# Gated cross-attention with a quantised feed-forward on one core: contexts in another row order, hand-written closing lists, and a different order of the first loads

## The chip, the cores and the metric

The kernel runs on one core of a Trainium2 chip. The metric is the device time of one launch in microseconds.

## What is computed

For 32 batches, queries `x` [32, 112, 256] attend to contexts `ctx_1024` [32, 375, 256], and a feed-forward with ternary weights and 8-bit activations follows. Cut to what matters:

```python
q  = layernorm(layernorm(x)) @ Wq * (1 + side) + side      # 16 heads of 64
k, v = split(layernorm(ctx) @ Wkv)
x  = x + tanh(g_xattn) * softmax(q k^T / 8) v @ Wout
h  = gelu(bitlinear(layernorm(x), w1, b1))
x  = x + tanh(g_ffn) * bitlinear(h, w2, b2)
# bitlinear: rmsnorm, activations rounded to 8 bits by the row's maximum, weights to -1, 0, 1
```

The softmax and the sum over the keys do not depend on the order of the 375 context rows.

## The kernel before

Products that need more than half precision are split into a high and a low f16 part, and `three` (L755 to L760) adds three products. Each batch goes through these steps, whose names are those of the order tables:

- LD, LX (SP): load the context into `ctx_in` [125, 3, 256] and the queries into `x_in` [112, 256]. BA, BB, BS (VectorE): their statistics; LNA (POOL): the scales; LNW (ScalarE): the normalised rows.
- Z0, Z1, ZX (TensorE): transposes into a work bank; ZF, ZXF (ScalarE) and ZS, ZXS (POOL): the high and low parts.
- K0 to K7, V00 to V12, Q0, Q1 (TensorE): projections, each into one of three PSUM work banks that go round in the order of TensorE's list. KH and VH (ScalarE) write the high part, KL and VL (VectorE) the low part and free the bank; QF (ScalarE) and QS (POOL) do it for the queries.
- For each of 8 pairs of heads: S (TensorE) scores, M (VectorE) maximum, E (ScalarE) exponential, PH (ScalarE or VectorE) high part, PL (POOL) low part, T (SP) the DMA transpose `pt<-pn`, A (TensorE) probabilities times values. N (VectorE) normalises four heads.
- OO, OH, OT: transpose the attention output and split it.

The 3584 rows of all batches are then taken as 28 tiles of 128 rows, numbered 0 to 27: WO (output projection), X1 and XST (residual, statistics), RM1, SC1, XR, XQ (quantise), XD (SP, DMA transpose of `xq`), XTE (VectorE, clips), F0 and F1 (first feed-forward product), HE0 and HE1, GE (gelu), SQ, HMX (maximum), RM2, SC2, HR, HQ (quantise), HD (DMA transpose of `hid_q`), HTE (clips), F2, YE, ST (store). In the tables tile t is written as a batch number: 31 is tile 27, 30 is 26, 29 is 25, 28 is 24, 27 is 23.

No scheduler decides anything. Each engine runs the list that `sequence` (L139) makes: FIRST[engine] for the opening rounds, then ORDER[engine] once per batch with offsets, until the batches run out. An engine waits on semaphores in front of a step, and all that stands behind in its list waits too. SP's list is the order of all DMAs on the one queue. The weights are loaded on SP at the start; those needed later (wout, w1, w2, the biases and gates, 3.7 MB) are issued inside `load` for batch 1, right after its context.

Of the kernel before, what the change touches and what calls it, by code (L numbers as in the profile page):

```python
# [4 lines left out]
F16 = mybir.dt.float16  # L5
ALU = mybir.AluOpType
# [3 lines left out]
B, SQ, D = 32, 112, 256  # L10
# [3 lines left out]
P = 128  # L14
# [33 lines left out]
ORDER, FIRST = {}, {}  # L48
# [20 lines left out]
]  # L69
# [20 lines left out]
]  # L90
# [48 lines left out]
def sequence(engine):  # L139

    done = set(FIRST[engine])
    steps = FIRST[engine] + [(name, it + off) for it in range(START, END) for name, off in ORDER[engine]
                             if 0 <= it + off < B and (name, it + off) not in done]
    return [(name, b - b // 8 - 1 if name in TOKEN_STEPS else b) for name, b in steps if b % 8 or name not in TOKEN_STEPS]
# [26 lines left out]
def build(nc, x, ctx, fside, g_x, g_f, ln1w, ln1b, ln2w, ln2b, wq, wkv, wout, w1, b1, w2, b2, out):  # L171
    from contextlib import ExitStack
    with ExitStack() as st:
# [25 lines left out]
        ident = sb("ident", [P, P])  # L199
# [70 lines left out]
        def _(sp):  # L270
            sp.dma_start(ctx_in[:], ctx[0].rearrange("(t p) d -> p t d", p=TP)).then_inc(ctx_loaded, 16)
# [11 lines left out]
            def load(b):  # L283
                if b == 0:
                    return
                sp.wait_ge(ctx_normed, b)
                sp.dma_start(ctx_in[:], ctx[b].rearrange("(t p) d -> p t d", p=TP)).then_inc(ctx_loaded, 16)
                if b == 1:
                    sp.dma_start(gates[:, 0:1], g_x.partition_broadcast(P)).then_inc(small_in, 16)
                    sp.dma_start(gates[:, 1:2], g_f.partition_broadcast(P)).then_inc(small_in, 16)  # L290
                    sp.dma_start(b2_row[:], b2.partition_broadcast(P)).then_inc(small_in, 16)
                    sp.dma_start(wout_f, wout.rearrange("(k p) n -> p k n", p=P)).then_inc(wout_in, 16)
                    sp.dma_start(w1_f, w1.rearrange("(k p) n -> p k n", p=P)).then_inc(w1_in, 16)
                    sp.dma_start(w2_f, w2.rearrange("(k p) n -> p k n", p=P)).then_inc(w2_in, 16)
                    sp.dma_start(b1_row[:], b1.partition_broadcast(P)).then_inc(small_in, 16)
# [30 lines left out]
            for name, b in sequence("SP"):  # L326
                if name[0] == "T":
                    turn(b, int(name[1]))
                if name == "XD":
                    turn_quantised(b)  # L330
                if name == "HD":
                    turn_hidden(b)
                if name == "LD":
                    load(b)
# [571 lines left out]
```

## Time and profile before

| | us |
|---|---|
| median of 3 runs | 1146.59 (1146.12 to 1147.98) |
| the profiled execution | 1148.09 |
| its span in the profile | 1146.2 |
| TensorE busy (93% of the span) | 1069.4 |
| ScalarE, VectorE, POOL busy | 974.0, 943.3, 776.7 |

The profile's span runs from the first to the last instruction of one execution; the profiled execution's own time is 1.9 us more. Busy time of TensorE counts matmuls with modelled ends. A row of a timeline gives the start, the duration, the engine, the line of the kernel, the operation, what is written and read, and in brackets how long the engine had been idle and what ended that.

### The profile page before, as it was taken

What the parts mean: (1) busy time and instruction counts of PE and PEld (TensorE: products, weight loads), DVE (VectorE), ACT (ScalarE), POOL (GpSimd) and SP (SyncE); (2) the same over time, 40 slices, a digit from 0 to 9 for tenths busy, and PEclk for the clock granted to TensorE, in tenths of its full rate; (3) what the DMA queues carried; (4) which work ended last, traced back from release to release, by engine and by line L of the source; (5) the groups of instructions that cost most, each with busy time, mean ns of one, the idle gap of its engine ahead of it and who ended that gap; (6) DMA issues with size and microseconds to landing.
All of it is one profiled execution on the core that took longest, in us unless ns stands there. A gap on an engine that the chain in (4) does not pass through costs nothing.

```text
span 1146.2 us, 32095 instructions
## 1 busy us (share of the span) xinstructions
PE 1069.4 (93%) x11890; PEld 735.4 (64%) x11890; DVE 943.3 (82%) x2108; ACT 974.0 (85%) x1866; POOL 776.7 (68%) x837
## 2 busy tenths in 40 slices
PE   3788999999999999999999999999999999999972
PEld 1455666776676676767666676776677667766650
DVE  3686788888889888888888878888988878988863
ACT  4677789999999979999999979999999979998861
POOL 3466577776767777676777666767777776777631
PEclk9899999999999999999999999999999999999975
DMA  8155745676786656778865776676667676755451
GB/s 273 50 97 91 115 87 108 125 114 113 117 137 108 103 113 124 117 108 125 119 111 110 127 115 104 112 136 101 111 126 114 117 122 111 120 107 103 105 103 30
DMA packets 418840, 129.72 MB, mean 113 GB/s; under 512 B 392480, under 2 KB 417536, under 8 KB 418688
## 3 DMA queue, kind: packets, MB, share of 16 engines
q1 hardware_dynamic: 418688, 127.68, 63.5%
q8 instruction: 97, 1.59, 0.6%
q14 instruction: 55, 0.45, 0.1%
HBM read 26.71 MB, written 3.67 MB: 27 GB/s over the span
## 4 chain that ended last, share of the span: by engine, by line
PE 71%; ACT 9%; DMA 6%; issue 6%; POOL 3%; DVE 3%; POOLq 1%; SPq 0%; DVEq 0%; ACTq 0%
PE work L757 15%; PE work L759 14%; PE work L758 14%; PE ps_s L776 10%; DMA pt<-pn 6%; PE ps_o L757 3%; PE ps_o L759 3%; PE ps_o L758 3%; ACT prob L538 2%; PE work L839 2%; PE work L857 2%; ACT L538 2%; ACT q_f L504 2%; PE work L863 2%; PE work L830 2%
## 5 line engine op out<-in xcount | busy, mean ns | idle before, releaser
L379 POOL TENSOR_TENSOR pn<-prob,pn 112x750 f16<-112x750 f32 x256 | 399.5, 1566 | 123.1 <-ACT pn L548 111.6
L538 ACT ACTIVATE prob<-ps_s,neg_max 112x375 f32<-112x375 f32 x512 | 265.2, 573 | 16.7 <-DVE neg_max L680 13.6
L680 DVE TENSOR_REDUCE neg_max<-ps_s 112x2 f32<-112x750 f32 x256 | 237.4, 928 | 23.6 <-PE ps_s L776 23.5
L757 PE MATMUL ps_o<-v_h,pt 128*128 128x65 f16 (+1 forms) x1536 | 168.3, 195 | 18.3 <-DMA pt<-pn 14.6
L757 PE MATMUL work<-z,wkv_h 128*128 128x375 f16 x512 | 168.6, 329 | 15.2 <-DVE k_l L605 8.1
L461 ACT ACTIVATE k_h<-work 128x375 f16<-128x375 f32 x256 | 121.4, 487 | 61.2 <-PE work L759 55.6
L605 DVE SCALAR_TENSOR_TENSOR k_l<-work,k_h 128x375 f16<-128x375 f32 x256 | 136.3, 540 | 40.7 <-ACT k_h L461 40.5
L758 PE MATMUL ps_o<-v_l,pt 128*128 128x65 f16 (+1 forms) x1536 | 168.0, 193 | 0.0
L759 PE MATMUL ps_o<-v_h,pt 128*128 128x65 f16 (+1 forms) x1536 | 168.0, 194 | 0.0
L759 PE MATMUL work<-z,wkv_l 128*128 128x375 f16 x512 | 167.4, 327 | 0.0
L758 PE MATMUL work<-z,wkv_h 128*128 128x375 f16 x512 | 167.0, 326 | 0.0
L757 PEld LDWEIGHTS ps_o<-v_h,pt 128*128 128x128 f16 (+1 forms) x1536 | 143.8, 98 | 34.1 <-DMA pt<-pn 18.7
L758 PEld LDWEIGHTS ps_o<-v_l,pt 128*128 128x128 f16 (+1 forms) x1536 | 143.2, 99 | 9.2
L757 PE MATMUL work<-wkv_h,z 128*128 128x512 f16 (+1 forms) x384 | 146.7, 382 | 1.4 <-DVE k_l L605 1.1
L759 PE MATMUL work<-wkv_h,z 128*128 128x512 f16 (+1 forms) x384 | 145.5, 379 | 0.0
L758 PE MATMUL work<-wkv_l,z 128*128 128x512 f16 (+1 forms) x384 | 145.4, 379 | 0.0
L759 PEld LDWEIGHTS ps_o<-v_h,pt 128*128 128x128 f16 (+1 forms) x1536 | 143.2, 97 | 0.0
L605 DVE SCALAR_TENSOR_TENSOR v_l<-work,v_h 128x512 f16<-128x512 f32 (+1 forms) x192 | 128.3, 681 | 6.7 <-ACT v_h L461 6.1
L461 ACT ACTIVATE v_h<-work 128x512 f16<-128x512 f32 (+1 forms) x192 | 115.6, 603 | 9.7 <-PE work L759 8.4
L548 ACT ACTIVATE pn<-prob 112x750 f16<-112x750 f32 x128 | 107.7, 842 | 0.1
L504 ACT ACTIVATE q_f<-work,side_add,side_mul 128x112 f32<-128x112 f32 x256 | 93.9, 467 | 6.0 <-PE work L759 6.0
L776 PE MATMUL ps_s<-k_h,q_h 64*112 64x375 f16 x512 | 88.7, 343 | 1.0 <-POOL q_l L387 0.7
(125 smaller groups left out, 2729.7 us busy)
## 6 DMA issues: line engine op xcount, KB each, us to landing
ctx_in<-in_ctx SPq DMA_DIRECT2D x32, 375.0 KB
pt<-pn SPq DMA_TRANSPOSE x256, 3.5
x_in<-in_x SPq DMA_DIRECT2D x32, 112.0 KB, 3.4
x_res<-in_x SPq DMA_DIRECT2D x28, 128.0 KB, 4.1
out<-y SPq DMA_DIRECT2D x28, 128.0 KB, 2.0
stage<-in_wkv SPq DMA_DIRECT2D x2, 1024.0 KB, 9.6
stage<-in_w SPq DMA_DIRECT2D x2, 1024.0 KB, 11.8
stage<-in_wq SPq DMA_DIRECT2D x1, 1024.0 KB, 9.1
```

Source lines behind the costliest of these rows:

```text
L379: g.tensor_tensor(buf[:, 1, :, 0:SK], prob[:, p % 2], buf[:, 0, :, 0:SK], ALU.subtract).then_inc(p_lo, 1)
L461: a.activation(dst, src, ACT.Identity, scale=1.0 / W_SCALE).then_inc(hi_done, 1)
L504: i = a.activation(q_f[:, c, :], work[:, BANK[job], m * SQ:(m + 1) * SQ], ACT.Identity, bias=add, scale=mul)
L538: i = a.activation(prob[:, p % 2, h, :], ps_s[0:SQ, 2 * (p % 2) + h, 0:SK], ACT.Exp, bias=neg_max[:, 2 * (p % 2) + h:2 * (p % 2) + h + 1])
L548: a.activation(pn[g % PBUF][:, 0, :, 0:SK], prob[:, p % 2], ACT.Identity).then_inc(p_hi_act, 1)
L605: v.scalar_tensor_tensor(out=dst, in0=src, scalar=1.0 / W_SCALE, in1=hi_part, op0=ALU.mult, op1=ALU.subtract).then_inc(evacuated[BANK[job] ...
L680: v.tensor_reduce(neg_max[:, 2 * (p % 2):2 * (p % 2) + 2], ps_s[0:SQ, 2 * (p % 2):2 * (p % 2) + 2, 0:SK], X, ALU.max, negate=True).then_in ...
L757: t_.matmul(dst, sh, mh, start=(n == 0), stop=False)
L758: t_.matmul(dst, sh, ml, start=False, stop=False)
L759: i = t_.matmul(dst, sl, mh, start=False, stop=(n == len(pairs) - 1))
L776: i = t_.matmul(ps_s[0:SQ, 2 * (p % 2) + h, 0:SK], q[r, p, :], k[r, p, :], start=(n == 0), stop=(n == 2))
L830: i = t_.transpose(w[:, t * TP:(t + 1) * TP], ctx_n[:, t, c * P:(c + 1) * P], ident[0:TP, 0:TP])
```

## The change

Five edits:

1. A context is loaded with three rows to a partition (row 3p + t in partition p, one piece of 3 KB) where partition p held rows p, 125 + p and 250 + p (three pieces of 1 KB).
2. The late weights are issued behind the queries of batch 1. The new list has LX of batch 1 ahead of LD of batch 1.
3. New FIRST lists for all five engines.
4. A LAST list for each engine, which sets the order of the closing rounds step by step.
5. For the last tile alone, `xq` and `hid_q` are transposed by TensorE into a PSUM bank (XT, HT), with a new f16 identity, and VectorE clips out of PSUM. The DMA transposes XD and HD of this tile are gone.

```diff
-            sp.dma_start(ctx_in[:], ctx[0].rearrange("(t p) d -> p t d", p=TP)).then_inc(ctx_loaded, 16)
+            sp.dma_start(ctx_in[:], ctx[0].rearrange("(p t) d -> p t d", p=TP)).then_inc(ctx_loaded, 16)
...
+            def load_queries(b):
+                if b > 0:
+                    sp.wait_ge(ctx_normed, b)
+                    sp.dma_start(x_in[:], x[b]).then_inc(x_loaded, 16)
                 if b == 1:
+                    load_late_weights()
...
-    done = set(FIRST[engine])
+    done = set(FIRST[engine] + LAST[engine])
     steps = FIRST[engine] + [(name, it + off) for it in range(START, END) for name, off in ORDER[engine]
-                             if 0 <= it + off < B and (name, it + off) not in done]
+                             if 0 <= it + off < B and (name, it + off) not in done] + LAST[engine]
...
+LAST["PE"] = [
...
+    ("K6", 31), ("A6", 30), ("F2", 27), ("A7", 30), ("S6", 31), ("S7", 31), ("OO1", 30), ("V01", 31),
+    ("V00", 31), ("WO", 30), ("F0", 29), ("F1", 29), ("V11", 31), ("A0", 31), ("V12", 31), ("V10", 31),
+    ("A1", 31), ("A2", 31), ("A3", 31), ("A4", 31), ("A5", 31), ("F2", 28), ("A6", 31), ("A7", 31),
+    ("OO0", 31), ("OO1", 31), ("F0", 30), ("F1", 30), ("WO", 31), ("F2", 29), ("XT", 31), ("F0", 31),
+    ("F1", 31), ("F2", 30), ("HT", 31), ("F2", 31),
+]
...
-                if name == "XTE":
+                if name == "XTE" and b == NT - 1:
+                    dve.wait_ge(full[BANK["XT", b]], USE["XT", b])
+                    v.tensor_scalar(xqt[:].rearrange("p c q -> p (c q)"), work[:, BANK["XT", b], :].bitcast(F16)[:, 0:KC * P],
+                                    -QMAX - 1, QMAX, ALU.max, ALU.min).then_inc(evacuated[BANK["XT", b]], 1)
...
+                if name == "XT":
+                    pe.wait_ge(xq_ready, b + 1)
+                    for c in range(KC):
+                        i = t_.transpose(wh[:, c * P:(c + 1) * P], xq[:, c * P:(c + 1) * P], ident_h[:])
+                if name == "HT":
+                    pe.wait_ge(hq_ready, b + 1)
+                    for c in range(FF // P):
+                        i = t_.transpose(wh[:, c * P:(c + 1) * P], hid_q[:, c * P:(c + 1) * P], ident_h[:])
```

How the instructions move, at three places. First, SP's opening, before:

```order
L281 DMA stage<-in_wkv 128x2x1024
L320 DMA x_res<-in_x 128x256
L287 DMA ctx_in<-in_ctx 125x3x256
L289 DMA gates<-in_g_x 128x1
L290 DMA gates<-in_g_f 128x1
L291 DMA b_row<-in_b 128x256
L292 DMA stage<-in_wout 128x8x256
L293 DMA stage<-in_w 128x2x1024
L294 DMA stage<-in_w 128x8x256
L295 DMA b_row<-in_b 128x1024
L337 DMA x_in<-in_x 112x256 x2
```

and now:

```order
L340 DMA stage<-in_wkv 128x2x1024
L350 DMA x_in<-in_x 112x256
L355 DMA gates<-in_g_x 128x1
L356 DMA gates<-in_g_f 128x1
L357 DMA b_row<-in_b 128x256
L358 DMA stage<-in_wout 128x8x256
L359 DMA stage<-in_w 128x2x1024
L360 DMA stage<-in_w 128x8x256
L361 DMA b_row<-in_b 128x1024
L345 DMA ctx_in<-in_ctx 125x768 x2
L350 DMA x_in<-in_x 112x256
```

The queries of batch 1 went ahead of the late weights, its context behind them, and the first `x_res` further back.

Second, VectorE's close, before: from the residual of the last tile (X1, L714) to its clipped transpose (L722). L737 is HMX and the first `clip` to `qs` (L642 to L649) is SC2, both of tile 26.

```order
L714 SCALAR_TENSOR_TENSOR x<-work,tanh_xs,x_res 128x256
L737 TENSOR_REDUCE amax<-stage 128x1
L630 BN_STATS x_bn<-x 128x6
L632 BN_AGGR x_mv<-x_bn 128x2
L634 TENSOR_SCALAR x_ve<-x_mv 128x1
L635 TENSOR_SCALAR xc<-x,x_mv 128x256
L637 TENSOR_REDUCE amax<-xc 128x1
L642 TENSOR_SCALAR clip<-amax,g_rs 128x1
L644 RECIPROCAL inv<-clip 128x1
L645 TENSOR_SCALAR deq<-clip,w_mean 128x1
L648 TENSOR_SCALAR deq2t<-deq,tanh_f 128x1
L649 SCALAR_TENSOR_TENSOR qs<-inv,g_rs 128x1
```

and now, from the scales of the last tile (SC1) to the last HMX:

```order
L717 SCALAR_TENSOR_TENSOR qs<-inv,x_c 128x1
L813 TENSOR_REDUCE amax<-stage 128x1
L821 SCALAR_TENSOR_TENSOR y<-work,deq2t,stage 128x256
L790 TENSOR_SCALAR xqt<-work 128x256
L710 TENSOR_SCALAR clip<-amax,g_rs 128x1
L712 RECIPROCAL inv<-clip 128x1
L713 TENSOR_SCALAR deq<-clip,w_mean 128x1
L716 TENSOR_SCALAR deq2t<-deq,tanh_f 128x1
L717 SCALAR_TENSOR_TENSOR qs<-inv,g_rs 128x1
L809 SCALAR_TENSOR_TENSOR stage<-work,deq,b_row 128x512 x2
L803 TENSOR_SCALAR stage<-hqt_r 128x1024
L813 TENSOR_REDUCE amax<-stage 128x1
```

HMX (L813) and SC2 of tile 26 now stand behind the scales of tile 27, and HTE of tile 26 (L803) stands ahead of the last HMX.

Third, TensorE's close, behind the last A7, before (L857 is F0 or F1, L839 is OO1, L863 is F2, and the rows from L757 on are WO):

```order
L857 MATMUL work<-w_t,xqt 128x512 x2
L839 MATMUL work<-ident,attn 128x112 x4
L857 MATMUL work<-w_t,xqt 128x512 x2
L863 MATMUL work<-w_t,stage 128x256 x8
L757 MATMUL work<-wout_h,stage 128x256
```

and now, from the last row of WO on (L931 is XT, L935 is HT):

```order
L835 MATMUL work<-wout_h,stage 128x256
L954 MATMUL work<-w_t,stage 128x256 x8
L931 MATMUL work<-ident_h,xq 128x128 x2
L945 MATMUL work<-w_t,xqt 128x512 x4
L954 MATMUL work<-w_t,stage 128x256 x8
L935 MATMUL work<-ident_h,stage 128x128 x8
L954 MATMUL work<-w_t,stage 128x256 x8
```

F2 of tile 25 moved from in front of WO to behind it, and the transposes of the last tile are TensorE's.

## Rows read from the trace of the kernel before

**Rows 1.** The page, busy time of each engine.
```profile
PE 1069.4 (93%) x11890; PEld 735.4 (64%) x11890; DVE 943.3 (82%) x2108; ACT 974.0 (85%) x1866; POOL 776.7 (68%) x837
```

**Rows 2.** Table of stretches: us, busy of each engine, granted clock, DMA share, GB/s.
```profile
0.00:60.00 60.00, 32.75 (x216) 19.04 (x217) 30.98 (x62) 31.95 (x56) 25.13 (x52) 0.91 0.52 157
60.00:150.00 90.00, 80.27 (x886) 53.18 (x885) 69.53 (x132) 67.58 (x137) 57.70 (x55) 0.98 0.59 99
150.00:1080.00 930.00, 922.30 (x10458) 639.85 (x10456) 806.43 (x1830) 845.54 (x1632) 669.88 (x705) 1.00 0.67 115
1080.00:1103.00 23.00, 16.78 (x218) 12.10 (x218) 20.38 (x41) 17.35 (x30) 15.18 (x15) 0.98 0.60 111
1103.00:1110.00 7.00, 4.32 (x58) 3.65 (x58) 2.81 (x10) 2.36 (x4) 3.62 (x4) 0.50 0.70 131
...
1118.00:1147.00 29.00, 5.72 (x22) 2.50 (x20) 9.73 (x29) 5.18 (x6) 5.20 (x9) 0.58 0.13 30
```

**Rows 3.** Waits of TensorE, 0 to 150 us: total, times, longest.
```profile
PE work L757 <- DVE k_l L605: 9.1, 3, 6.6
...
PE ps_o L757 <- DMA pt<-pn: 4.8, 3, 2.6
```

**Rows 4.** Timeline of the opening: SP, VectorE and TensorE.
```profile
22.92 14.68 SPq L337 DMA_DIRECT2D x_in<-in_x  x2
...
32.41 0.43 DVE L702 BATCH_NORM_STATS2 ln_bn<-x_in 112x6 f32<-112x256 f32 x1 [5.55 <-DMA x_in<-in_x]
...
34.63 0.49 PE L757 MATMUL work<-z,wkv_h 128*128 128x375 f16 x1 [6.63 <-DVE k_l L605]
```

**Rows 5.** DMA view of 37.6 to 42.6 us, 40 slices: busy tenths of 16 engines, GB/s.
```profile
DMA  0000058677411100023333333333333332333323
GB/s 0 0 0 0 0 98 164 197 246 221 90 41 57 25 0 0 33 98 123 123 123 123 123 123 123 123 115 123 115 123 123 123 123 106 123 123 115 123 98 115
```

**Rows 6.** Waits of TensorE, 1080 to 1147 us.
```profile
PE work L857 <- DVE xqt L722: 12.2, 3, 10.0
...
PE ps_o L757 <- DMA pt<-pn: 4.0, 4, 1.4
PE ps_o L757 <- issue: 3.2, 1, 3.2
```

**Rows 7.** Timeline of TensorE: end of S7, start of A7, last F2.
```profile
1093.10 0.32 PE L776 MATMUL ps_s<-k_h,q_l 64*112 64x375 f16 x2
...
1108.54 0.24 PE L757 MATMUL ps_o<-v_h,pt 128*128 128x65 f16 x1 [1.35 <-DMA pt<-pn]
...
1141.30 1.86 PE L863 MATMUL work<-w_t,stage 128*128 128x256 f16 x8 [9.05 <-DVE stage L727]
```

**Rows 8.** Timeline of ScalarE: one table load, the last HR.
```profile
1093.91 1.28 ACT L559 ACT_TABLE_LOAD   x1
...
1135.24 1.24 ACT L567 ACTIVATE stage<-stage,round_col,qs 128x1024 f32<-128x1024 f32 x1 [2.02 <-DVE qs L649]
```

**Rows 9.** Timeline of VectorE: X1, HMX, the last XTE and HTE.
```profile
1118.26 0.48 DVE L714 SCALAR_TENSOR_TENSOR x<-work,tanh_xs,x_res 128x256 f32<-128x256 f32 x1 [2.61 <-PE work L759]
1118.66 1.21 DVE L737 TENSOR_REDUCE amax<-stage 128x1 f32<-128x1024 f32 x1
...
1127.73 0.23 DVE L722 TENSOR_SCALAR xqt<-xqt_r 128x256 f16<-128x256 f16 x1 [4.22 <-DMA xqt_r<-xq]
...
1140.72 0.43 DVE L727 TENSOR_SCALAR stage<-hqt_r 128x1024 f16<-128x1024 f16 x1 [5.52 <-DMA hqt_r<-stage]
```

**Rows 10.** Timeline of SP: the last XD and HD.
```profile
1125.41 1.17 SPq L309 DMA_TRANSPOSE xqt_r<-xq  x1
...
1137.64 1.23 SPq L315 DMA_TRANSPOSE hqt_r<-stage  x1
```

**Rows 11.** Groups on POOL: the low part of the probabilities; the last HQ.
```profile
L379 POOL TENSOR_TENSOR pn<-prob,pn 112x750 f16<-112x750 f32 x256 | 399.5, 1566 | 123.1 <-ACT pn L548 111.6
...
1136.57 1.05 POOL L441 TENSOR_SCALAR stage<-stage 128x1024 f16<-128x1024 f32 x1 [2.39 <-ACT stage L567]
```

More of the change, by code:

```diff
@@ L33 @@
 CAST_ACT = (0, 2, 4, 6)
-ORDER, FIRST = {}, {}
+ORDER, FIRST, LAST = {}, {}, {}
 ORDER["PE"] = [
@@ L77 @@
 FIRST["ACT"] = [
[9 rows of a table removed]
+    ("LNW", 0), ("WKH", 0), ("ZF1", 0), ("ZF0", 0), ("ZXF", 0), ("WQH", 0), ("KH1", 0), ("WVH", 0),
[8 rows of a table added]
     ("LNW", 3), ("KH3", 2), ("E4", 1), ("OH1", 0), ("PH4", 1), ("VH12", 1), ("E5", 1), ("QF0", 2),
[1 row of a table removed]
[1 row of a table added]
     ("E7", 1), ("VH00", 2), ("VH02", 2), ("E0", 2), ("VH01", 2),
+]
+LAST["ACT"] = [
[11 rows of a table added]
 ]
@@ L99 @@
 FIRST["DVE"] = [
[9 rows of a table removed]
[9 rows of a table added]
+]
+LAST["DVE"] = [
[14 rows of a table added]
 ]
@@ L115 @@
 FIRST["POOL"] = [
[5 rows of a table removed]
[5 rows of a table added]
+]
+LAST["POOL"] = [
[6 rows of a table added]
 ]
@@ L126 @@
 FIRST["SP"] = [
[3 rows of a table removed]
[3 rows of a table added]
     ("T7", 1), ("T0", 2), ("T1", 2), ("LD", 5), ("T2", 2), ("T3", 2), ("LX", 5), ("T4", 2),
[2 rows of a table removed]
[2 rows of a table added]
+]
+LAST["SP"] = [
[5 rows of a table added]
 ]
@@ L197, in build @@
         w1_t, w2_t = sb("w1_t", [P, KC, FF], F16), sb("w2_t", [P, FF // P, D], F16)
-        ident = sb("ident", [P, P])
+        ident, ident_h = sb("ident", [P, P]), sb("ident_h", [P, P], F16)
         ones, minus_half, round_col = sb("ones", [P, P]), sb("minus_half", [P, 4]), sb("round_col", [P, 1])
@@ L281, in _, with load_context, load_late_weights @@
             sp.dma_start(wkv_f[:, :, INNER:2 * INNER], wkv_v[:, :, INNER:2 * INNER]).then_inc(wv_in, 16)
[L283 to L287, printed above, removed]
-                if b == 1:
[L289 to L295, printed above, removed]
+            def load_context(b):
+                if b > 0:
+                    sp.wait_ge(ctx_normed, b)
+                    sp.dma_start(ctx_in[:], ctx[b].rearrange("(p t) d -> p t d", p=TP)).then_inc(ctx_loaded, 16)
+            def load_queries(b):
+                if b > 0:
+                    sp.wait_ge(ctx_normed, b)
+                    sp.dma_start(x_in[:], x[b]).then_inc(x_loaded, 16)
+                if b == 1:
+                    load_late_weights()
+            def load_late_weights():
+                sp.dma_start(gates[:, 0:1], g_x.partition_broadcast(P)).then_inc(small_in, 16)
+                sp.dma_start(gates[:, 1:2], g_f.partition_broadcast(P)).then_inc(small_in, 16)
+                sp.dma_start(b2_row[:], b2.partition_broadcast(P)).then_inc(small_in, 16)
+                sp.dma_start(wout_f, wout.rearrange("(k p) n -> p k n", p=P)).then_inc(wout_in, 16)
+                sp.dma_start(w1_f, w1.rearrange("(k p) n -> p k n", p=P)).then_inc(w1_in, 16)
+                sp.dma_start(w2_f, w2.rearrange("(k p) n -> p k n", p=P)).then_inc(w2_in, 16)
+                sp.dma_start(b1_row[:], b1.partition_broadcast(P)).then_inc(small_in, 16)
             def turn(b, p):
@@ L328, in _ @@
                     turn(b, int(name[1]))
-                if name == "XD":
+                if name == "XD" and b < NT - 1:
                     turn_quantised(b)
-                if name == "HD":
+                if name == "HD" and b < NT - 1:
                     turn_hidden(b)
                 if name == "LD":
-                    load(b)
-                if name == "LX" and b > 0:
-                    sp.wait_ge(ctx_normed, b)
-                    sp.dma_start(x_in[:], x[b]).then_inc(x_loaded, 16)
+                    load_context(b)
+                if name == "LX":
+                    load_queries(b)
                 if name == "RS":
@@ L350, in _ @@
             g.memset(ident[:], 0.0)
+            g.memset(ident_h[:], 0.0)
             g.memset(ln_mv[:], 1.0)
@@ L353, in _ @@
             pool.drain()
-            g.affine_select(out=ident[:], in_=ident[:], compare_op=ALU.not_equal, fill=1.0, base=0,
-                            pattern=[[-1, P]], channel_multiplier=1).then_inc(consts_ready, 1)
+            for t in (ident, ident_h):
+                i = g.affine_select(out=t[:], in_=t[:], compare_op=ALU.not_equal, fill=1.0, base=0,
+                                    pattern=[[-1, P]], channel_multiplier=1)
+            i.then_inc(consts_ready, 1)
             g.memset(v_h[:, :, :, DH:VW], 1.0)
@@ L719, in step @@
                     scales(x1_rms, b, amax1, x1_c, clip1, inv1, qs1, deq1, 0)
-                if name == "XTE":
+                if name == "XTE" and b == NT - 1:
+                    dve.wait_ge(full[BANK["XT", b]], USE["XT", b])
+                    v.tensor_scalar(xqt[:].rearrange("p c q -> p (c q)"), work[:, BANK["XT", b], :].bitcast(F16)[:, 0:KC * P],
+                                    -QMAX - 1, QMAX, ALU.max, ALU.min).then_inc(evacuated[BANK["XT", b]], 1)
+                if name == "HTE" and b == NT - 1:
+                    dve.wait_ge(full[BANK["HT", b]], USE["HT", b])
+                    v.tensor_scalar(hqt[:].rearrange("p c q -> p (c q)"), work[:, BANK["HT", b], :].bitcast(F16)[:, 0:FF // P * P],
+                                    -QMAX - 1, QMAX, ALU.max, ALU.min).then_inc(evacuated[BANK["HT", b]], 1)
+                if name == "XTE" and b < NT - 1:
                     dve.wait_ge(x_turned, 16 * (b + 1))
                     v.tensor_scalar(xqt[:], xqt_r[:], -QMAX - 1, QMAX, ALU.max, ALU.min).then_inc(x_clipped, 1)
-                if name == "HTE":
+                if name == "HTE" and b < NT - 1:
                     dve.wait_ge(h_turned, 16 * (b + 1))
@@ L798, in job @@
                 w = work[:, bank, :]
+                wh = w.bitcast(F16)
                 if USE[name, b] > 1:
@@ L853, in job @@
                         pe.wait_ge(tern_ready[0], 1)
-                    pe.wait_ge(x_clipped, b + 1)
+                    if b == NT - 1:
+                        results(b, ["XT"])
+                    else:
+                        pe.wait_ge(x_clipped, b + 1)
                     c = slice(int(name[1]) * HALF, (int(name[1]) + 1) * HALF)
@@ L860, in job @@
                         pe.wait_ge(tern_ready[1], 1)
-                    pe.wait_ge(h_clipped, b + 1)
+                    if b == NT - 1:
+                        results(b, ["HT"])
+                    else:
+                        pe.wait_ge(h_clipped, b + 1)
                     for c in range(FF // P):
```

120 rows, old and new, of the table CAST_ACT are left out of this document.

## The prediction

> **What bounds the kernel now.** I read the page first. TensorE is busy for 1069.4 us of a span of 1146.2 [rows 1]. The table of stretches then says where the missing 76.8 us are [rows 2]. Between 150 and 1080 us TensorE is busy for 922.3 of 930 us, so the rounds in the middle are TensorE's own work, and the change does not touch their order. The first 150 us hold 27.2 + 9.7 = 36.9 us of idle TensorE, and the stretch from 1080 us to the end holds 32. Everything that this change can win or lose lies in these two ends.
>
> At the start, the waits of TensorE name a K evacuation on VectorE as the longest one after the first load: 9.1 us in three waits, one of them 6.6 [rows 3]. Its origin is a load. SP issues the second batch's queries at 22.92 us, behind 3.7 MB of late weights, and VectorE idles 5.55 us for them until 32.41 [rows 4]. VectorE takes its work in order, so K evacuations stand behind that wait, all three work banks stay full, and TensorE stops.
>
> At the end there are two kinds of idle time. Up to the last probability-times-value pair (A7 of batch 31, which starts at 1108.54 [rows 7]) TensorE waits 4.0 us for transposed probabilities, 3.2 us for "issue", and some 1.4 us for other things, 8.6 in all [rows 6]; the granted clock then falls to 0.50, the lower of its levels (1.2 GHz) [rows 2]. Behind it stands one serial chain for the last token tile, from its output projection (X1 starts at 1118.26 [rows 9]) to 1146.2, 28 us in which TensorE works 5.7 [rows 2].
>
> **The closing list up to A7.** Before, the scores S6 and S7 of batch 31 end about 1093.4 and A7 starts 15.1 us later [rows 7]. Only F2, WO and A0 to A5 are left to fill that time, so TensorE runs dry, and ScalarE loads a table of functions twice inside it, 1.28 us each [rows 8]. The list puts work back there: behind S6, S7 now stand OO1, V01, V00, WO, F0, F1, V11, A0, V12, V10, A1 to A5 and F2, and the scores come some 12 us earlier for it. No work disappears. What can be won is the idle time, 8.6 us, and what the half clock cost the 4.32 us of work between 1103 and 1110 [rows 2], at most 2.2 us and by my estimate 1.3, since not all of these instructions run at the speed of the columns. From this I take 0.9 us for F2 of tile 24, which now stands ahead of A6 (eight matmuls that take 1.86 at the low clock [rows 7], half of it here), and a remaining stall of 2. The stall is real because the chain from S7 to A7 is still long: table load 1.28 [rows 8], two exponentials, the cast, POOL's subtraction of 1.57 us [rows 11], HR and HQ of tile 24 (1.24 and 1.05 [rows 8, 11]), and on SP the transpose of tile 24's hidden row, which is queued ahead of T7. I add these up to about 17 us, and the cover behind S7 to about 14.5. Sum: 8.6 + 1.3 - 0.9 - 2.0 = **7.0 us**. Bounds: 0 (ScalarE is busy 17.35 of 23 us and VectorE 20.38 of 23 in the stretch before 1103 [rows 2]; if VectorE's order is the limit, nothing is won) and 9.9.
>
> **From A7 to the end of WO.** Before, F0 of tile 26 stands ahead of OO1, and F1 of 26 and F2 of 25 stand ahead of WO. F2 of 25 alone is 1.86 at the low clock. Now OO1 follows the last normalisation at once and F2 stands behind WO, but F0 and F1 of 26 still stand ahead of it and VectorE has XTE of 26 ahead of its last OT. I take **1.6 us**, bounds 0 and 2.9 (F2's 1.86 and one F0 of about 1).
>
> **From WO to the end.** Let WO end at T, so that X1 starts at T + 0.1. Before, the maximum over tile 26 (HMX, 1.21 us [rows 9]) and its scales run ahead of the last tile's statistics and scales, and HR and HQ of 26 ahead of XR and XQ: by the closing rows this is 1.1 + 0.9 + 0.9 us. All four now stand behind. Then xq was turned by a DMA: 1125.41 to 1127.96 with the clip, 2.55 us [rows 9, 10]. Now it is two TensorE transposes and a clip from PSUM. No row has an f16 transpose. Two of the eight F2 matmuls (twice as many columns) take 0.47, so 0.23 to 0.47 for the pair, and the clip of 256 elements 0.23 (its row from SBUF) to 0.48 (X1's, from PSUM). I take 0.65 in all, but XTE stands behind HMX and YE of older tiles on VectorE, which gives back 0.9. So F0 of the last tile starts about T + 5.7 where it started at T + 9.8.
>
> Then comes what is late next. VectorE's last list has HTE of tile 26 ahead of HMX of 27. Tile 26's scales now come after XTE of 27, at T + 6.4; its HR (1.24), HQ (1.05) [rows 8, 11] and a DMA transpose of 3.1 us, read from 1137.64 to 1140.72 [rows 9, 10], put HTE at T + 12 to 12.4. F2 of 26 (1.86) and YE follow, and both stand ahead of the last SC2. It starts at about T + 14.9; before, it started at T + 16.1. So of the 4.1 us won by then, 3 are lost again, in the wait of VectorE for the hidden transpose.
>
> Last, hq was turned in 3.51 us with its clip [rows 9, 10]. Now it is eight transposes, 0.93 (half of F2's 1.86) to 1.86, I take 1.2; and the clip of 1024 elements from PSUM, 0.43 (its row from SBUF) to 1.21 (HMX's row, 1024 elements at one input per cycle), I take 1.2 because a PSUM operand is nearer to the second. Gain 1.1, bounds 0.4 and 2.2. Sum for this part: 1.2 + 1.1 = **2.3 us**, bounds 0.5 and 6.5 (no stall).
> The Trainium skill (VectorE: DVE Perf Modes, The three transpose paths) gives 390 ns for one 128x128 transpose on TensorE. It speaks against the second of these edits: eight of them would be 3.1 us by an estimate from that page, and the path through PSUM would be slower than the DMA by 0.8 us instead of faster by 1.1. I go by the matmul row, because in it the eight are pipelined.
>
> **The start.** Three changes meet. First, contexts come as 125 pieces of 3 KB instead of 375 of 1 KB. A context load that has the queue to itself runs at 115 to 123 GB/s with 0.3 of the 16 DMA engines busy [rows 5]. Pieces of 3 KB leave the number of partitions at 125, so I expect the same share and at most a tenth more speed, 0.4 us of about 3.3 per load. The loads are covered by a whole round in the middle, so this is worth 0 to 1 us over the run; I take **0.3**.
> The Trainium skill (DMA: Bandwidth & Descriptors, Why a DMA increments its semaphore by 16 and not by 1) says that the outermost size sets the number of engines, the largest divisor up to 16, which for 125 is 5 of 16 in either layout; by it too the new layout buys no more engines.
>
> Second, the queries of batch 1 are issued first, then the 3.7 MB, and only then its context. The wait does not go, it changes its name: VectorE's BA of batch 1 now stands for the context, ahead of KL1. The bytes ahead of the last load are the same less x_res (128 KB, moved behind), so I put the landing at 31.4 us, where the queries came at 32.4. BA, KL1 and the rest of the statistics then put the last statistic some 0.6 us later than now. TensorE gets its bank back at about 32.7 instead of 34.63 [rows 4], but has done three K jobs by then instead of four, and a K job takes about as long as this difference at the low clock. So this part is **0**, bounds -1.5 (gain) and +3 (the context comes at 34 instead). Third, the opening lists are new. They aim at the some 10 us of idle time between 60 and 105 us (9.7 in the stretch from 60 to 150 [rows 2], 4.8 before it and in it for transposed probabilities [rows 3]). I cannot tell by reading how much they win. I take **1.5 us**, bounds -2 and 6.
>
> **The sum.** 7.0 + 1.6 + 2.3 + 0.3 + 0 + 1.5 = 12.7 us. The profiled execution took 1148.09 with its span of 1146.2; the median of the runs is 1146.59. The sum is a difference of spans, so I take it from the median: 1133.9, say **1134 us**.
>
> **The rivals.**
> *A, full closing gain.* The walk to A7 keeps up (9 us), HTE of 26 is early enough so that the stall of 3 us does not appear, and the opening wins 4: 1146.6 - 9 - 2 - 5.3 - 4.3 = 1126. For it: the idle time is there to be taken. Against it: three engines are near their limit, VectorE above all.
> *B, the closing list wins only its last part.* VectorE, or SP's in-order queue, sets the pace up to A7 and the start gives nothing: 3.9 us for the parts behind A7 and up to 2 before it, 1141 us. For it: SP works strictly in order, and T7 stands behind a transpose that needs HQ of tile 24, which POOL does after its last subtraction.
> *C, the wrong side.* The context of batch 1 is issued last and stands in front of every K evacuation. If the five busy DMA engines have it only at 40 us or later, TensorE loses 8 us with its clock down, and batch 1's scores move by as much, and with B at the end the result is 1146.6 + 8 - 5 = 1149.6. It decides from a landing near 40 us together with a closing gain under 6. Against it: 3.7 MB were through by 32.4 in the trace of before.
> *D, the change cancels out*: a start that loses 5 us against a closing gain of 5, 1146.6.
> *E, the last transposes do not pipeline*: each of the ten waits for the one before to leave the array, as a single short PV matmul does in its row (0.24 us [rows 7]), and a little more for twice its columns, 0.3 to 0.4. Then XT costs 0.4 us more and HT 1.2 to 2.0: 1136. For it: no row shows an f16 transpose. Against it: the F2 row. It is the rule of the Trainium skill named above, as a mechanism here.
>
> **How the numbers follow.** Forecast (1129 to 1138) 0.46, E 0.09 (inside the same range), A 0.17, B 0.18, D 0.05, C 0.05. The range leaves out C, D and the far side of A: 1125 to 1143. Differences under 0.2% (2.3 us) are about what a measurement of this kernel can't tell from none. Faster by more: 0.90. Within: 0.05. Slower: 0.05.
>
> **What would show it.** Right: A7's last matmul ends near 1102 (in the span), the stretch before it has under 3 us of idle TensorE, the last F0 starts within 6 us of the end of WO, VectorE waits about 5 us for hqt_r between HE1 and HMX of the last tile, and from WO to the end there are about 25.6 us instead of 28. At the start VectorE waits for ctx_in where it waited for x_in, until 31 to 32 us. The middle is unchanged, with TensorE busy for 99% of it. Wrong: more than 6 us of idle TensorE between the last scores and A7, eight transposes with their clip of more than 3.5 us, or a context that lands after 35 us.

## The result, and the profile after

The changed kernel takes 1128.07 us (median of 4 runs, 1127.29 to 1132.53) against 1147.24 for the kernel before on the same chip. The ratio is 0.9839, with a 95% interval of 0.9825 to 0.9854: 18.5 us faster by the ratio, where I had forecast 12.7. Run again later beside other kernels it had 1129.76 us and 0.9852 [0.9832, 0.9872], 17.0 us. The profiled execution is the slowest of the first four, 1132.53 us with a span of 1130.7; the second profile has a span of 1128.0, and from the last A7 on its positions lie some 3 us earlier. One of the four executions of the kernel with the closing edits alone took 2768.28 us where the other three took 1134.15 to 1135.37; its ratio leaves it out.

The page of the changed kernel, part 1: busy time, share and instructions of each engine. It answers to [rows 1].

```profile
PE 1067.6 (94%) x11900; PEld 733.8 (65%) x11900; DVE 945.4 (84%) x2108; ACT 970.6 (86%) x1864; POOL 776.6 (69%) x839
```

No work went: TensorE is busy 1.8 us less than before, and the rest is idle time taken out. The stretches of the changed kernel, whose columns are those of [rows 2]:

```profile
0.00:60.00 60.00, 30.30 (x218) 18.09 (x220) 30.55 (x60) 30.74 (x55) 25.83 (x51) 0.89 0.50 155
60.00:105.00 45.00, 40.52 (x442) 26.31 (x439) 38.95 (x70) 37.78 (x74) 29.34 (x30) 1.00 0.56 105
105.00:150.00 45.00, 43.74 (x504) 29.92 (x504) 35.06 (x73) 34.51 (x73) 31.44 (x31) 1.00 0.65 102
150.00:1050.00 900.00, 893.98 (x10142) 619.91 (x10139) 782.97 (x1774) 821.53 (x1591) 655.23 (x692) 1.00 0.68 115
1102.00:1130.70 28.70, 11.16 (x64) 6.41 (x62) 12.62 (x34) 7.94 (x10) 7.15 (x11) 0.63 0.15 38
```

And the kernel before, in the same two stretches of the opening:

```profile
60.00:105.00 45.00, 36.68 (x415) 24.04 (x413) 37.38 (x67) 36.59 (x73) 30.47 (x28) 1.00 0.57 94
105.00:150.00 45.00, 43.59 (x471) 29.13 (x472) 32.16 (x65) 30.99 (x64) 27.23 (x28) 0.96 0.60 103
```

The reader sees where the opening won: from 60 to 105 us TensorE was idle for 8.3 us and is now for 4.5. From 105 to 150 its work is the same. The first 60 us got worse (30.30 us busy against 32.75 [rows 2]). These are the waits of TensorE in the first 150 us, to be read against [rows 3]:

```profile
PE work L907 <- ACT x_n L597: 13.1, 1, 13.1
PE work L833 <- DVE k_l L673: 8.7, 2, 7.7
PE work L833 <- POOL z L468: 5.6, 1, 5.6
PE work L833 <- DVE v_l L673: 3.0, 2, 2.3
PE work L907 <- DVE k_l L673: 2.2, 1, 2.2
PE ps_o L833 <- DMA pt<-pn: 1.3, 1, 1.3
```

The rows with `k_l` (8.7 and 2.2 us) all fall in the first 60 us, where the kernel before waited 6.6 us for K evacuations. The long one is still there, 7.7 us instead of 6.6, and VectorE's timeline shows that only its cause was renamed, as forecast:

```profile
31.68 0.75 DVE L766 BATCH_NORM_STATS2 ln_bn<-ctx_in 125x6 f32<-125x256 f32 x2 [10.10 <-DMA ctx_in<-in_ctx]
32.35 0.53 DVE L673 SCALAR_TENSOR_TENSOR k_l<-work,k_h 128x375 f16<-128x375 f32 x1
```

VectorE idles 10.10 us for the context of batch 1, which SP issued at 21.21 us behind the late weights. Waits for transposed probabilities fell from 4.8 us to 1.3.

In the close I follow three marks: the end of A7 of batch 31, the end of WO of the last tile (T), and the end of the span.

| | end of A7 | end of WO | end of span |
|---|---|---|---|
| before | 1109.7 | 1118.1 | 1146.2 |
| after, first profile | 1099.3 | 1105.2 | 1130.7 |
| after, second profile | 1096.6 | 1102.4 | 1128.0 |

A7 to WO shrank from 8.4 to 5.9 us, WO to the end from 28.1 to 25.6. Behind WO, TensorE's timeline of the changed kernel (first profile), to be read against [rows 7]:

```profile
1108.37 1.03 PE L954 MATMUL work<-w_t,stage 128*128 128x256 f16 x8 [3.21 <-DVE stage L803]
1110.39 0.37 PE L931 MATMUL work<-ident_h,xq 128*128 128x128 f16 x2 [0.99 <-POOL xq L496]
1111.24 1.87 PE L945 MATMUL work<-w_t,xqt 128*128 128x512 f16 x4 [0.47 <-DVE xqt L790]
1118.19 1.86 PE L954 MATMUL work<-w_t,stage 128*128 128x256 f16 x8 [5.08 <-DVE stage L803]
1124.24 1.01 PE L935 MATMUL work<-ident_h,stage 128*128 128x128 f16 x8 [4.18 <-POOL stage L509]
1126.12 1.87 PE L954 MATMUL work<-w_t,stage 128*128 128x256 f16 x8 [0.87 <-DVE stage L794]
```

and VectorE's and SP's, to be read against [rows 9, 10]:

```profile
1110.80 0.29 DVE L790 TENSOR_SCALAR xqt<-work 128x256 f16<-128x256 f16 x1 [0.16 <-PE work L931]
1111.19 0.21 DVE L710 TENSOR_SCALAR clip<-amax,g_rs 128x1 f32<-128x1 f32 x1
...
1114.53 1.23 SPq L381 DMA_TRANSPOSE hqt_r<-stage  x1
...
1117.62 0.43 DVE L803 TENSOR_SCALAR stage<-hqt_r 128x1024 f16<-128x1024 f16 x1 [3.72 <-DMA hqt_r<-stage]
1117.96 1.21 DVE L813 TENSOR_REDUCE amax<-stage 128x1 f32<-128x1024 f32 x1
1120.19 0.48 DVE L821 SCALAR_TENSOR_TENSOR y<-work,deq2t,stage 128x256 f32<-128x256 f32 x1 [1.02 <-PE work L954]
1120.77 0.21 DVE L710 TENSOR_SCALAR clip<-amax,g_rs 128x1 f32<-128x1 f32 x1
...
1125.29 0.69 DVE L794 TENSOR_SCALAR stage<-work 128x1024 f16<-128x1024 f16 x1 [3.60 <-PE work L935]
```

F0 of the last tile starts at T + 6.1. VectorE then waits 3.72 us for tile 26's hidden transpose, and only after its YE (1120.19) come the last tile's scales, at T + 15.6.

### The profile page after: what moved, and what is told of

Its sections match the earlier page's. It is cut to its first block, busy times and chain, and to the rows that moved or that the text cites. A ratio compares the mean times of both kernels' runs of the same rounds, so it can differ in the third digit from the quotient of the medians.

```text
span 1130.7 us, 32113 instructions
## 1 busy us (share of the span) xinstructions
PE 1067.6 (94%) x11900; PEld 733.8 (65%) x11900; DVE 945.4 (84%) x2108; ACT 970.6 (86%) x1864; POOL 776.6 (69%) x839
## 4 chain that ended last, share of the span: by engine, by line
PE 73%; ACT 8%; issue 5%; DMA 4%; DVE 4%; POOL 3%; POOLq 1%; DVEq 1%; SPq 0%; ACTq 0%
PE work L833 15%; PE work L834 15%; PE work L835 15%; PE ps_s L852 10%; DMA pt<-pn 4%; PE ps_o L833 3%; PE ps_o L835 3%; PE ps_o L834 3%; ACT prob L606 2%; PE work L916 2%; PE work L945 2%; ACT q_f L572 2%; PE work L907 2%; PE work L954 2%; ACT L606 2%
```

## The experiments

Twelve kernels in three calls. Each call had its own runs of the kernel before (medians 1147.65, 1147.28, 1147.84), so I compare by ratios, and within one profile by distances from T. A microsecond is 0.0009 of ratio; the intervals are 1 to 3 us to each side, so differences of about 2 us between two changed kernels rest on the traces more than on the ratios.

**1. The change taken apart.** The new layout alone, in the kernel before:

```diff
-            sp.dma_start(ctx_in[:], ctx[0].rearrange("(t p) d -> p t d", p=TP)).then_inc(ctx_loaded, 16)
+            sp.dma_start(ctx_in[:], ctx[0].rearrange("(p t) d -> p t d", p=TP)).then_inc(ctx_loaded, 16)
```

> The kernel before, with the contexts laid out as three rows to a partition in pieces of 3 KB and nothing else. Theory (the closing lists carry the change): the same as before within 1 us; the context load alone still keeps 0.3 of the DMA engines busy. Rival (the layout carries a good part): 3 us or more faster, with most of it in the stretch from 150 to 1080 us.

Measured: 1145.19 us, ratio 0.9979 [0.997, 0.9988], 2.4 us faster. Eight times my 0.3, and outside "within 1 us", though short of the rival's 3. The rival had the place right: in the profile, X1 of the second tile starts 0.5 us earlier than before (170.4 us against 170.9) and X1 of tile 24 2.0 us earlier (1030.9 against 1032.9), so most of the gain gathers in the middle rounds.

The opening with the layout, without the closing lists:

```diff
-LAST["PE"] = [
-    ("Q0", 30), ("Q1", 30), ("A2", 29), ("K5", 30), ("A3", 29), ("K4", 30), ("Z1", 31), ("A4", 29),
...
+LAST["PE"] = []
```

> The changed kernel without its closing lists, and with the last tile turned by DMA as before: layout, late weights behind the queries, new opening lists. Theory: 1 to 4 us faster than before, from the stretch between 60 and 150 us, and from its last 80 us on the same times as before. Rival (the opening carries it): 8 us or more faster.

Measured: 1141.42 us, ratio 0.9948 [0.9935, 0.9961], 6.0 us faster: more than my 1 to 4, less than the rival's 8.

And the closing edits alone (the changed kernel with the old FIRST lists, the old order of loads and the old layout):

```diff
-                    sp.dma_start(ctx_in[:], ctx[b].rearrange("(p t) d -> p t d", p=TP)).then_inc(ctx_loaded, 16)
+                    sp.dma_start(ctx_in[:], ctx[b].rearrange("(t p) d -> p t d", p=TP)).then_inc(ctx_loaded, 16)
+                if b == 1:
+                    load_late_weights()
...
-                if b == 1:
-                    load_late_weights()
```

> The kernel before with the closing lists and the last tile turned by TensorE; old layout, old opening lists, old order of loads. Theory: 13 to 17 us faster than before, so that this and the opening add up to the whole change of about 19. Rival (the two overlap): under 11 us, or more than 18.

Measured: 1135.08 us (1134.78 without the long execution), ratio 0.9891 [0.9876, 0.9906], 12.5 us faster, just under my 13 to 17 and over the rival's 11; in its trace A7 ends at 1101.5, WO at 1107.4 and the span at 1133.0. Opening 6.0 and closing 12.5 make 18.5, the whole as first measured (17.0 the second time): within the intervals the two ends add up. X1 of tile 24 starts at 1032.7 us in this trace and at 1032.9 before, so the closing edits win nothing ahead of it.

**2. The order of the first loads.** The changed kernel with the context of batch 1, then the late weights, then the queries, as before:

```diff
-    ("LX", 1), ("LD", 1), ("LD", 2), ("LX", 2), ("T0", 0), ("T1", 0), ("T2", 0), ("LX", 3),
+    ("LD", 1), ("LX", 1), ("LD", 2), ("LX", 2), ("T0", 0), ("T1", 0), ("T2", 0), ("LX", 3),
```

(and `load_late_weights` called from `load_context`).

> The changed kernel, its new lists kept, with the loads in the order of before: the context of batch 1, the late weights, its queries. Theory (the swap of the two loads is worth nothing): within 1.5 us of the changed kernel. Rival (the queries in front win by themselves): 2 us or more slower than the changed kernel.

Measured: 1129.1 us, 0.9841 [0.9825, 0.9858], the same as the changed kernel (0.9839). Which of the two loads stands behind the weights is worth nothing that shows here.

That none of them stands there is another matter. Both loads of batch 1 ahead of the late weights, in the changed kernel (`load_late_weights` called from `load_context`, with LX of batch 1 still first):

> The changed kernel with the late weights issued behind both the queries and the context of batch 1 (before: the context, the weights, the queries; changed: the queries, the weights, the context). Theory (a load behind 3.7 MB sets the resume of TensorE at 33 us, whichever load it is): the wait of 7.7 us for the K evacuation goes, the context lands before 25 us, 4 to 7 us faster than the changed kernel. Rival (the late weights are needed then and take the wait over, or the lists fit only the old landing): under 2 us faster.

Measured: 1120.64 us, 0.976 [0.9738, 0.9781]: 9 us faster than the changed kernel, more than the 4 to 7 that I expected. Its stretches:

```profile
0.00:60.00 60.00, 35.40 (x293) 22.14 (x295) 38.25 (x71) 37.11 (x69) 32.62 (x59) 0.97 0.63 170
60.00:105.00 45.00, 43.11 (x488) 28.15 (x485) 38.68 (x72) 39.03 (x76) 30.53 (x30) 1.00 0.59 115
```

TensorE works 5.1 us more in the first 60 us and 2.6 us more from 60 to 105; the granted clock of the first stretch is 0.97 instead of 0.89. VectorE takes up the context at 21.66 us, where the changed kernel does at 31.68:

```profile
21.66 0.74 DVE L766 BATCH_NORM_STATS2 ln_bn<-ctx_in 125x6 f32<-125x256 f32 x2
23.34 0.55 DVE L673 SCALAR_TENSOR_TENSOR k_l<-work,k_h 128x375 f16<-128x375 f32 x1 [0.95 <-ACT k_h L529]
```

Is this the load alone, or the new lists with it? The same in the kernel before, with its own lists and pieces (the seven late loads leave `load` and stand behind the queries of batch 1):

```diff
             for name, b in sequence("SP"):
...
                 if name == "LX" and b > 0:
                     sp.wait_ge(ctx_normed, b)
                     sp.dma_start(x_in[:], x[b]).then_inc(x_loaded, 16)
+                    if b == 1:
+                        sp.dma_start(gates[:, 0:1], g_x.partition_broadcast(P)).then_inc(small_in, 16)
...
```

> The kernel before with its own lists and 1 KB pieces; only the 3.7 MB of late weights are issued behind the second batch's queries and not ahead of them, so that neither the context nor the queries of batch 1 stand behind them. Theory (the wait for a load behind the weights is the opening's main loss in either kernel): 6 to 10 us faster than the kernel before, since VectorE's 5.55 us wait for the queries and TensorE's 6.6 us wait go, and more ahead of it. Rival (the 9 us of the other kernel with early loads come from the new lists, which want the context early): 0 to 3 us faster.

Measured: 1142.22 us, 0.9956 [0.9942, 0.9969], 5.1 us: between the theory's 6 to 10 and the rival's 0 to 3. The old lists can use about half of it: TensorE is busy 37.11 us from 60 to 105 us, hardly more than before, where the new lists reach 43.11. So the early load is worth some 5 us by itself, and the rest needs the lists.

**3. The layout in the changed kernel.** The changed kernel with 1 KB pieces again:

```diff
-            sp.dma_start(ctx_in[:], ctx[0].rearrange("(p t) d -> p t d", p=TP)).then_inc(ctx_loaded, 16)
+            sp.dma_start(ctx_in[:], ctx[0].rearrange("(t p) d -> p t d", p=TP)).then_inc(ctx_loaded, 16)
```

> The changed kernel with the contexts in 375 pieces of 1 KB again. In the kernel before, the 3 KB layout alone was worth 2.4 us where I had forecast 0.3. Theory (the gain comes from shorter context loads that contend less with the transposes of probabilities, in all rounds): this kernel is 2 to 3 us slower than the changed kernel. Rival (the gain belongs to the old opening, where VectorE waited for those loads; the new lists and the order of loads would hide it or make more of it): under 1 us, or, since batch 1's context is now the last load of the opening and all else waits for it, over 4 us.

and, as its measure, the changed kernel itself:

> The changed kernel unaltered, once more, as the measure for the other kernels of this call. Its four runs so far spread from 1127.3 to 1132.5 us. Both theories expect a ratio to the kernel before of 0.983 to 0.985.

Measured: 1133.81 us and 0.9877 [0.9861, 0.9893] against 1129.76 and 0.9852 [0.9832, 0.9872]: 2.9 us by the ratios, 4.0 by the medians, with intervals that overlap; the two profiled spans differ by 1.6. Together with the 2.4 us in the kernel before, the theory of a gain over all rounds fits, and a gain that belongs to one opening does not. The waits of the middle rounds, 150 to 1050 us, show the same in both pairs. In the kernel before, then with the new layout:

```profile
DVE x L714 <- DMA x_res<-in_x: 15.7, 14, 1.7
...
PE ps_o L757 <- DMA pt<-pn: 5.8, 10, 0.9
```

```profile
DVE x L714 <- DMA x_res<-in_x: 4.9, 6, 1.2
...
PE ps_o L757 <- DMA pt<-pn: 4.8, 6, 1.2
```

In the changed kernel with 1 KB pieces, then with 3 KB (second profile):

```profile
DVE x L782 <- DMA x_res<-in_x: 15.7, 14, 1.7
...
PE ps_o L833 <- DMA pt<-pn: 5.4, 10, 1.0
```

```profile
DVE x L782 <- DMA x_res<-in_x: 7.5, 8, 1.4
...
PE ps_o L833 <- DMA pt<-pn: 3.8, 5, 0.9
```

What gets shorter is not the context load, which nobody waits for in the middle, but the waits of others: the residual tiles for VectorE and the transposed probabilities for TensorE. SP's own rows show where it starts. The order behind a context load is the same in both kernels: a transpose, the residual tile, a transpose. Before, then with the new layout:

```profile
428.50 3.87 SPq L302 DMA_TRANSPOSE pt<-pn  x1
432.43 0.58 SPq L320 DMA_DIRECT2D x_res<-in_x  x1
```

```profile
427.57 1.81 SPq L302 DMA_TRANSPOSE pt<-pn  x1
429.43 0.58 SPq L320 DMA_DIRECT2D x_res<-in_x  x1
```

In the 22 middle rounds with this order SP is busy issuing this transpose for 3.2 to 4.1 us with pieces of 1 KB (median 3.7) and for 1.3 to 2.2 with 3 KB (median 2.0); the changed kernel's pair shows medians of 3.8 and 2.1. The residual tile is issued 1.8 us earlier after the context, and takes 5.2 us to land instead of 4.4. The transpose behind it takes SP 3.4 us instead of 1.8, so most of the lead ends there. TensorE's idle time from 150 to 1050 us falls from 7.7 to 6.3 us, 1.4 us of the 2.1 by which the two profiled spans differ. Why SP needs less time behind larger pieces, and how the lead passes on to TensorE, no run shows.

**4. The last tile's transposes.** Both back on the DMA queue, in the changed kernel:

```diff
-    ("OO0", 31), ("OO1", 31), ("F0", 30), ("F1", 30), ("WO", 31), ("F2", 29), ("XT", 31), ("F0", 31),
-    ("F1", 31), ("F2", 30), ("HT", 31), ("F2", 31),
+    ("OO0", 31), ("OO1", 31), ("F0", 30), ("F1", 30), ("WO", 31), ("F2", 29), ("F0", 31),
+    ("F1", 31), ("F2", 30), ("F2", 31),
...
-    ("HD", 30), ("ST", 30), ("ST", 31),
+    ("XD", 31), ("HD", 30), ("ST", 30), ("HD", 31), ("ST", 31),
```

> The changed kernel with the two transposes of the last tile given back to the DMA; all lists the same otherwise. Theory: 1.5 to 3 us slower than the changed kernel; the first transpose loses about 2 us but much of that disappears in the wait for the hidden row of the tile before (it ends at the same time in both), the second loses 1.3 to 1.8. Rival (each counts in full): 4 us slower.

Measured: 1134.91 us, 0.9895 [0.9879, 0.991]; 6.4 us slower than the changed kernel by its first ratio, 4.9 by the later one; the changed kernel did not run in the same call. Its trace gives the size more sharply: from T to the end 29.95 us instead of 25.5, so 4.4. My theory of 1.5 to 3 fails and the rival (each counts in full) holds. VectorE's timeline, with T at 1102.85:

```profile
1111.33 0.23 DVE L798 TENSOR_SCALAR xqt<-xqt_r 128x256 f16<-128x256 f16 x1 [2.78 <-DMA xqt_r<-xq]
1111.65 0.21 DVE L710 TENSOR_SCALAR clip<-amax,g_rs 128x1 f32<-128x1 f32 x1
...
1118.07 0.43 DVE L803 TENSOR_SCALAR stage<-hqt_r 128x1024 f16<-128x1024 f16 x1 [3.71 <-DMA hqt_r<-stage]
...
1121.22 0.21 DVE L710 TENSOR_SCALAR clip<-amax,g_rs 128x1 f32<-128x1 f32 x1
...
1127.63 0.43 DVE L803 TENSOR_SCALAR stage<-hqt_r 128x1024 f16<-128x1024 f16 x1 [5.49 <-DMA hqt_r<-stage]
```

VectorE waits 3.71 us for the hidden row of tile 26 here as well. All that stands behind XTE of the last tile (1111.33, T + 8.5; in the changed kernel T + 5.6) came later by the same: tile 26's scales, its HR, HQ and HD, its HTE at T + 15.2 instead of T + 12.5. So the time that XT saves arrives in full, since the chain that VectorE then waits for starts behind XTE.

Only the hidden row back on the DMA queue:

> Only the last hidden row is turned by a DMA again; the quantised row of the last tile stays on TensorE. With both by DMA the stretch from WO's end to the end was 4.4 us longer, of which I ascribe 2.7 to the quantised row and 1.7 to the hidden row. Theory: this kernel is 1.7 us (1.2 to 2.2) slower than the changed kernel of this call, and the stretch from WO's end to the end is 27.2 us instead of 25.5. Rival: the whole stretch hangs on the hidden row and the quantised row's gain is lost in VectorE's wait for tile 26, as my prediction has it; then this kernel is 3.5 us or more slower.

Measured: 1131.96 us, 0.9865 [0.9849, 0.9881] beside 0.9852, 1.5 us slower by the ratios, whose intervals overlap, and 2.2 by the medians; from T to the end 27.15 us against 25.56, 1.6. The theory holds and its rival (3.5 or more) falls: of the 4.4 us, HT is worth 1.6 and XT 2.8.

**5. The wait for tile 26.** The last tile gets a scale column of its own, so that its scales can be written before YE of tile 26 has read the old ones:

```diff
-    ("HE1", 31), ("HTE", 30), ("HMX", 31), ("YE", 30), ("SC2", 31), ("HTE", 31), ("YE", 31),
+    ("HE1", 31), ("HMX", 31), ("SC2", 31), ("HTE", 30), ("YE", 30), ("HTE", 31), ("YE", 31),
...
-                v.tensor_scalar(deq2t[:], deq2[:], tanh_f[:], None, ALU.mult)
+                v.tensor_scalar((deq2u if b == NT - 1 else deq2t)[:], deq2[:], tanh_f[:], None, ALU.mult)
```

(and POOL waits for tile 26's DMA transpose before it writes the last hidden row.)

> The changed kernel with the stall near the end taken out: the last tile has its own output scale, so that on VectorE its maximum and scales (HMX, SC2) can stand ahead of the clip and output of the tile before (HTE, YE). Theory (VectorE waits 3.7 us for the hidden row of tile 26 and TensorE's F2 of 26 adds to it): 2.5 to 3.8 us faster than the changed kernel. Rival (the chain is bound by gelu and square anyway): under 1 us.

Measured: 1126.22 us, 0.9816 [0.9799, 0.9834], 2.6 us faster than the changed kernel by ratios whose intervals overlap; from T to the end 22.2 us instead of 25.5, so 3.3. Its VectorE rows, with T at 1102.04:

```profile
1114.19 0.21 DVE L712 TENSOR_SCALAR clip<-amax,g_rs 128x1 f32<-128x1 f32 x1 [1.00 <-POOL g_rs L506]
...
1118.71 0.69 DVE L796 TENSOR_SCALAR stage<-work 128x1024 f16<-128x1024 f16 x1 [0.63 <-PE work L937]
```

The last scales start at T + 12.2 instead of T + 15.6. That is the price of the stall which I had put at 3 us.

**6. The best version.** The early context and the scale column together:

> The changed kernel with both edits, the late weights behind queries and context of batch 1, and the last tile's own output scale. Theory (they lie at the two ends and add up): 7 to 10 us faster than the changed kernel, about 1119 us. Rival: the gain of one is lost in the other, under 6 us.

Measured: 1117.54 us, ratio 0.9735 [0.9712, 0.9759]. It is 30.4 us faster than the kernel before and 11.9 faster than the changed one by its first ratio, more than my 7 to 10; 9.1 and 2.6 by themselves make 11.7, so they add.

## Why the prediction was right, and where its size was not

The direction, the places and most of the mechanisms were right; the cause of the stall ahead of A7, the price of the layout and what becomes of XT's gain were not. The time of 1128.07 lies inside my range of 1125 to 1143, and the gain was 18.5 us instead of 12.7. Of the signs that I gave, two were missed: A7 ended at 1099.3 and 1096.6 in the two profiles instead of near 1102, and the last F0 started 6.1 us behind WO, not within 6. Term by term, the closing ones against the marks of the run with the closing edits alone:

| term | forecast | measured |
|---|---|---|
| up to the end of A7 | 7.0 | 8.2 |
| A7 to WO | 1.6 | 2.5 |
| WO to the end | 2.3 | 2.5 |
| layout | 0.3 | 2.4 |
| order of the first loads | 0 | 0 |
| opening lists | 1.5 | 3.6 (6.0 less 2.4) |
| sum | 12.7 | 19.2 by these, 18.5 by the ratio |

**Two terms were mis-sized, both away from the close: the layout and the opening lists**, 4.2 us of the 5.8 missing. The step of the layout reasoned that a context load has 0.3 of the DMA engines and 123 GB/s in either layout, and that the loads are covered by a whole round. Both hold: in the trace of the layout alone, the load that [rows 5] shows runs at 0.3 of the engines and about the same 123 GB/s.

```profile
DMA  0046489430111514332233333333333334311000
GB/s 0 0 49 106 106 279 287 156 33 0 49 74 74 123 49 123 98 98 98 98 123 147 123 123 147 123 123 123 123 123 123 123 147 172 123 74 49 0 0 0
```

What failed is the price of a hidden load read from a load at rest. In the middle rounds transposes and the residual tile stand behind it on SP, the first of them is issued in about 2.0 us instead of 3.7, and the waits for them fell. I had rows for this (the waits for transposed probabilities, four times in the close and three in the opening) and took them as given.

For the opening lists I wrote that I could not tell by reading, and took 1.5 from a place with about 10 us of idle time. The place was right and the measured gain of TensorE in it is 4.1 us (36.68 to 40.78 us busy from 60 to 105 us, opening edits alone, layout included):

```profile
60.00:105.00 45.00, 40.78 (x459) 26.82 (x457) 37.69 (x70) 39.44 (x77) 29.60 (x31) 1.00 0.56 105
```

The first 60 us give 2.4 of this back (30.38 us busy against 32.75), and the stretch to 150 adds 0.7. By X1 of the first tile, which started at 137.5 us before, the changed kernel is 3.8 and 3.2 us ahead in its two profiles. My upper bound of 6 holds for the 3.6. A middle value nearer to half of the idle time would have been no less founded than 1.5.

**Up to A7**, the close won 8.2. Until A7's end, idle TensorE fell by 5.8 us (53.3 to 47.5) and its busy time by 2.4 (1056.4 to 1054.0). I had 6.6 for the idle part and 0.4 for the clock less F2. The last stretch before A7's end, in the kernel with the closing edits alone, has the full clock where the kernel before had 0.50 [rows 2]:

```profile
1095.00:1101.54 6.54, 4.65 (x118) 4.39 (x119) 5.69 (x16) 3.29 (x5) 1.74 (x5) 1.00 0.58 125
```

So the clock gave more than I had priced. It does not always stay: in the first profile of the changed kernel, which has the same closing lists, it is 0.52 in the last 6.3 us before A7's end, and A7's short matmuls take 0.24 us there, where they take 0.19 in the second profile. That is a part of the 2.7 us by which the two profiles differ at A7; the rest I leave open.

The remaining stall has about the size that I gave it (2) and another cause. I put 2 us on the long chain to A7 with a transpose late on SP; in the changed kernel no wait of TensorE for a transpose is left there, and the stall is VectorE's. That the size came out is luck:

```profile
PE ps_o L833 <- DVE attn L682: 2.6, 2, 1.8
```

This is the normalisation of batch 31 that must free the accumulator.

**From WO to the end** I was within 0.3 us, with the steps nearly as written: F0 at T + 6.1 (forecast 5.7), HTE of tile 26 at T + 12.5 (12 to 12.4), the last scales at T + 15.6 (14.9), and a wait of 3.72 us of VectorE between HE1 and HMX, where I had said about 5. One sentence needs a correction. "Of the 4.1 us won by then, 3 are lost again" holds for the start of the last F0 against the start of the last scales. But it does not mean that XT's own gain drowns in the stall: dropping XT costs 2.8 us, the whole of it. The 3 us belong to the reordering, which put tile 26's scales and quantisation behind the last tile's, and the scale column takes them out.

The transposes cost 0.37 us for two and 1.01 for eight, where I had up to 0.47 and 1.2; the clips from PSUM 0.29 and 0.69, where I had 1.2 for the larger. Rival E, transposes that do not pipeline, falls with the eight in 1.01 us. The 390 ns that the Trainium skill (VectorE: DVE Perf Modes, The three transpose paths) gives for one transpose would have made 3.1, by an estimate from that page; this trace does not agree with it for transposes in a row.

**The first loads**: the wait changed its name and not its worth. The context was taken up at 31.68 us (forecast 31.4), the bank came back at 32.94 (32.7), and the kernel with the old order is as fast. Rival C, a context at 40 us or later, did not occur. Rival A's 1126 is nearer to the result than my 1134, and part of its story holds (more from the opening and from the walk to A7), but its missing stall is there. Rivals B and D fall: the walk to A7 kept up, and the opening won.

## What to carry to other kernels

Where a wait only changes its name, look for what both names stand behind: here 3.7 MB of weights that nobody needs yet, and issuing them behind both loads of batch 1 gave another 9 us, half as much as the whole change. Price a hidden transfer by what is issued behind it on its queue, not by whether somebody waits for it. And where a saving seems to vanish in a later wait, follow the chain that releases that wait: if it starts behind the place of the saving, the saving arrives.

## What the runs showed of the hardware

- Eight f16 128x128 transposes in a row on TensorE took 1.01 us, 0.126 each, at the lower granted clock, and two took 0.37. From the start of the first to the end of the clip it was 0.70 us for `xq` and 1.74 for `hid_q`.
- VectorE clipped 1024 f16 elements per partition out of PSUM in 0.69 us, against 0.43 from SBUF and 1.21 for the f32 maximum over as many.
- Contexts in 3 KB pieces instead of 1 KB took 8000 packets off the queue (418,688 to 410,688) and its share of the 16 engines from 63.5% to 62.4% of the span, with a lone load still at 0.3 of the engines and about 123 GB/s. In the middle rounds SP issued the DMA transpose right behind such a load in 2.0 us instead of 3.7 (medians of 22).
